# In the expert stage, TensorE's step goes from gate, up, weight spread, down to gate, weight spread, down, up

## The chip, the cores and the metric

The kernel runs on one core of a Trainium2 chip. The metric is the device time of one launch in microseconds (us), as the median of several runs. The profile is that of one execution on the same core.

## What is computed

Four layers follow each other, each added to its input x of 16 sequences, 128 rows and 256 columns: a grouped cross attention, a mixture of experts, a latent cross attention, and a feed-forward layer on quantised numbers. The change lies in the mixture of experts alone:

```python
logits = jnp.einsum('bsh,eh->bse', x, classifier_w)          # 12 routes, 8 of them experts
probs = softmax(logits)
_, idx = jax.lax.top_k(probs + e_score_correction_bias, 2)
rw = jnp.take_along_axis(probs, idx, axis=-1) * 1.5
w_full = jnp.sum(one_hot(idx, 12) * rw[..., None], axis=-2)
g = jnp.einsum('bsh,eih->bsei', x, gate_w)
u = jnp.einsum('bsh,eih->bsei', x, up_w)
expert_out = jnp.einsum('bsei,ehi->bseh', jax.nn.silu(g) * u, down_w)
out = jnp.einsum('bse,bseh->bsh', w_full[..., :8], expert_out)
out = out + x * jnp.sum(w_full[..., 8:], axis=-1, keepdims=True)
```

Here x is the normalised input of the layer.

## The kernel before

The function `routed_experts` holds the stage. Its work is cut into 32 units: 4 groups of 4 sequences (512 rows), and in each group the 8 experts. Unit u is expert x of group j, with u = 8j + x. A unit passes through all engines:

- TensorE makes the gate and the up product of the unit (L881), six matmuls of 512 columns each: two halves of the 256 columns, times three products, since every operand is split in a high and a low part.
- ScalarE takes the silu of the gate product (`gated`, L937). VectorE multiplies it with the up product (`inner`, L979).
- TensorE spreads the routing weight of this expert over the 128 partitions (L895). VectorE multiplies it in (`h`, L1008, in the helper `hidden`).
- ScalarE rounds h to its high part (`ht`, L945), GpSimd subtracts that to get the low part (`ht`, L1088).
- TensorE makes the down products (L904), 12 matmuls of 256 columns, which add up over the 8 experts of a group in `down_ps`. At the end of a group VectorE adds them to x (L1001).

The order of the work is written out by hand: each engine has a function `step(u, j, x)` and runs it for u = 0 to 34. Steps 0 to 7 are written out, steps 8 to 31 are a hardware loop over the groups, and three steps drain the pipeline. Each engine executes in this order and waits on semaphores. In step u TensorE makes gate and up of unit u, the spread of unit u - 2, the down products of unit u - 3, and in even steps three transposes of quantised weights for the last layer (L914). In step u VectorE makes `inner` of unit u - 1, then a piece of that quantisation, then `h` of unit u - 2. The piece is `block_powers` in an even step (four instructions, L1023 to L1027) and `shift` in an odd one (five instructions on 384 columns, L1034 to L1041). In step u GpSimd makes the low part of unit u - 3, then its piece of the quantisation (L1095 in even steps, L1099 in odd ones, the latter after `shift`), and then work for later stages: a rotation of the context in the steps with x = 0 to 4 (L1121 to L1131) and a scaling of x with x = 6 and 7 (L1072, L1075).

TensorE waits for these: `inner_made` before the gate product, so that the PSUM bank of unit u - 2 is free; `h_lo` (the low part) before the down products; `h_made` before the spread, since the spread's bank has only one copy. `inner` waits for `gated_made` and `up_made`.

The routing weights of a group have to be turned before they can be spread: `routes(g)` (L868) transposes them on TensorE into the spread's bank, ScalarE copies them (L929), VectorE subtracts for the low part (L968), and the spread waits for `w_lo`. This happens in step 1 for group 0 and in steps 3, 4 and 5 for groups 1 to 3, between the gate and the up product.

```python
if inside(u, UNITS):
    wait(pe, inner_made, u - 1)
    for w, out, made in ((0, gate_ps[par], gate_made), (2 * FFN, up_ps[par], up_made)):
        if first and u in (3, 4, 5) and made is up_made:
            routes(u - 2)
```

Of the kernel before, what the change touches and what calls it, by code (L numbers as in the profile page):

```python
# [24 lines left out]
B, S, E = 16, 128, 256  # L25
CE = 64
EPS = 1e-5
HALVES = E // 128
GROUPS = B // 4
PRODUCTS = ((0, 0), (0, 1), (1, 0))  # L30
# [10 lines left out]
EXPERTS, ZERO, INTER = 8, 4, 128  # L41
# [9 lines left out]
FFN, MX = 1024, 32  # L51
# [5 lines left out]
def wait(engine, semaphore, value):  # L57

    if isinstance(value, int) and value <= 0:
        return  # L60
    engine.wait_ge(semaphore, value)


def inside(n, count):

    return not isinstance(n, int) or 0 <= n < count
# [10 lines left out]
def run_of(ap, j, count=4):  # L77

    return ap.rearrange("p (j b) s -> p j b s", b=count)[:, j, :, :]
# [690 lines left out]
def routed_experts(nc, m, d):  # L770
# [7 lines left out]
    with ExitStack() as scope:  # L778
# [3 lines left out]
        UNITS = GROUPS * EXPERTS  # L782
# [7 lines left out]
        ht = [sb(f"ht{i}", [INTER, 2, N], F32R) for i in range(2)]  # L790
# [5 lines left out]
        gate_ps, up_ps = [m.bank(0), m.bank(2)], [m.bank(1), m.bank(3)]  # L796
        down_ps = m.ps[:, 4:6, :].rearrange("s c (b e) -> s (c b) e", b=2)
# [7 lines left out]
        w_at = lambda part, c, width: m.wsplit[:, part, c:c + width]  # L805
# [5 lines left out]
        gate_made, up_made, gated_made, inner_made = (sem(n) for n in ("e_gate", "e_up", "e_gated", "e_inner"))  # L811
        weight_spread, h_made, h_hi, h_lo, down_made = (sem(n) for n in ("e_weight", "e_h", "e_h_hi", "e_h_lo", "e_down"))
        x_made, parts_made, stats_made, var_made = (sem(n) for n in ("e_x", "e_parts", "e_stats", "e_var"))
# [11 lines left out]
        def steps(engine, step):  # L825

            def group(j):
                for x in range(EXPERTS):
                    step(EXPERTS * j + x, j, x)

            group(0)
            with engine.Fori(1, GROUPS) as j:
                group(j)
            for x in range(3):
                step(UNITS + x, GROUPS, x)

        @block.sync
        def _(sp):
            sp.dma_start(m.kv_cos[:, :], d["kv_cos"]).then_inc(m.rope_loaded, 16)
            sp.dma_start(m.kv_sin[:, :], d["kv_sin"]).then_inc(m.rope_loaded, 16)  # L840
            sp.dma_start(m.kvt_cos[:, :], d["kvt_cos"]).then_inc(m.rope_loaded, 16)
            sp.dma_start(m.kvt_sin[:, :], d["kvt_sin"]).then_inc(m.rope_loaded, 16)
            sp.dma_start(m.ctx_t[:, :, :, :], d["ctx_t"]).then_inc(m.rope_loaded, 16)
            sp.dma_start(m.rope[:, :, :], d["rope"]).then_inc(m.rope_loaded, 16)

            def load(c2, j, buf):

                wait(sp, mx_made, 2 * c2 - 2)
                sp.dma_start(raw[buf][:, :, :], d["mx"][c2, :, :, :]).then_inc(mx_loaded[buf], 16)

            load(0, 0, 0)
            load(1, 0, 1)
            with sp.Fori(1, GROUPS) as j:
                load(2 * j, j, 0)
                load(2 * j + 1, j, 1)
            load_wide(sp, m, d, 0)

        @block.tensor
        def _(pe):
            def routes(g):  # L860
                if g == 0:
                    pe.wait_ge(route, ROUTE_STEPS)
                else:
                    pe.wait_ge(h_made, g)
                if g == 3:
                    pe.wait_ge(mx_kept, 1)
                for s in range(4):
                    t = pe.transpose(weights_turned_ps[:, s * S:(s + 1) * S], weights[:, 4 * g + s, :], m.ident[:, :])  # L868
                t.then_inc(w_turned, 1)

            def step(u, j, x):
                par, old = x % 2, 1 - x % 2
                first = isinstance(u, int) and u < UNITS
                if inside(u, UNITS):
                    wait(pe, inner_made, u - 1)
                    for w, out, made in ((0, gate_ps[par], gate_made), (2 * FFN, up_ps[par], up_made)):
                        if first and u in (3, 4, 5) and made is up_made:
                            routes(u - 2)
                        for k in range(HALVES):
                            for q, (pw, py) in enumerate(PRODUCTS):  # L880
                                t = pe.matmul(out, w_at(pw, w + k * EXPERTS * INTER + x * INTER, INTER),  # L881
                                              run_of(m.yt[:, py, k, :, :], j).rearrange("p b s -> p (b s)"),
                                              start=(k == 0 and q == 0), stop=(k == HALVES - 1 and q == 2))
                        t.then_inc(made, 1)
                if first and u == 1:
                    routes(0)
                if inside(u - 2, UNITS):
                    if first and u == 2:
                        pe.wait_ge(m.selected, 1)
                    if first and 2 <= u <= 5:  # L890
                        pe.wait_ge(w_lo, u - 1)
                    wait(pe, h_made, u - 2)
                    if x % 2:
                        wait(pe, mx_kept, 4 * j + x // 2 - 1)
                    pe.matmul(weight_ps, select[:, (x - 2) % EXPERTS, :],  # L895
                              weights_t[:, j if x >= 2 else j - 1, :], start=True, stop=True).then_inc(weight_spread, 1)
                if inside(u - 3, UNITS):
                    expert = (x - 3) % EXPERTS
                    pe.wait_ge(h_lo, u - 2)
                    if expert == 0:  # L900
                        wait(pe, x_made, j)
                    for q, (ph, pw) in enumerate(PRODUCTS):
                        for s in range(4):
                            t = pe.matmul(down_ps[:, s, :], ht[old][:, ph, s * S:(s + 1) * S],  # L904
                                          w_at(pw, 4 * FFN + expert * E, E),
                                          start=(expert == 0 and q == 0 and s % 2 == 0),
                                          stop=(expert == EXPERTS - 1 and q == 2 and s % 2 == 1))
                    t.then_inc(down_made, 1)
                if x % 2 == 0 and inside(u - 2 - LEAD, UNITS):
                    c = 4 * j + x // 2 - 1  # L910
                    pe.wait_ge(mx_made, c)
                    pe.wait_ge(h_made, u - 1 if inside(u - 2, UNITS) else UNITS)
                    for i in range(3):
                        t = pe.transpose(mx_ps[:, i * 128:(i + 1) * 128],  # L914
                                         quantised[(x // 2) % 2][:, i * 128:(i + 1) * 128], m.ident16[:, :])
                    t.then_inc(mx_turned, 1)

            for b in range(B):
                t = pe.transpose(logit_ps[:, b, :], m.logits_t[:, b // 4, (b % 4) * S:(b % 4 + 1) * S],
                                 m.ident[0:ROUTES, 0:ROUTES])  # L920
            t.then_inc(logits_turned, 1)
            steps(pe, step)

        @block.scalar
# [1280 lines left out]
```

## Time and profile before

| | |
|---|---|
| median of 3 runs | 818.46 us (818.2 to 818.87) |
| the profiled execution's own time | 819.62 us |
| span of its profile, first to last instruction | 817.8 us |
| its mean granted TensorE clock | 0.981 |
| TensorE matmul busy | 749.2 us (92% of the span) |
| VectorE busy | 594.5 us (73%) |
| GpSimd busy | 567.1 us (69%) |
| ScalarE busy | 403.1 us (49%) |
| expert stage, first gate product to last transposes | 172.32 to 336.03 us |

The profiled execution took 1.16 us more than the median, and its span leaves 1.82 us around the first and the last instruction. Shares of the whole span say little on one stage; the stage is read in the trace from 172 to 337 us. In the rows, PE is TensorE's matmuls, PEld its weight loads, DVE is VectorE, ACT ScalarE, POOL GpSimd.

### The profile page before, as it was taken

How to read it: one execution, taken by the hardware profiler on the slowest of the kernel's cores; microseconds unless marked ns; L12 is line 12 of the kernel's file. 1: busy time of each engine (PE TensorE's matmuls, PEld its weight loads, DVE VectorE, ACT ScalarE, POOL GpSimd, SP SyncE). 2: the span in 40 equal slices, each digit the busy share in tenths (PEclk: the TensorE clock that was granted, in tenths of full speed). 3: DMA queues.
4: the chain of work that ended last, by engine and by line, in shares of the span. 5: the costliest groups of instructions: out<-in, count | busy, mean ns of one | idle time of the engine just before them, and what ended most of it. 6: DMA issues, size and time to landing. Idle time of an engine off the chain costs nothing. (4 is left out here: it accounts for less than half of the span.)

```text
span 817.8 us, 14830 instructions
## 1 busy us (share of the span) xinstructions
PE 749.2 (92%) x4801; PEld 538.7 (66%) x4808; DVE 594.5 (73%) x1087; ACT 403.1 (49%) x1068; POOL 567.1 (69%) x590
## 2 busy tenths in 40 slices
PE   3999999878999998789999999999999999876786
PEld 2555555457888887656877777777777777653464
DVE  5888889856777878656465575886678675749994
ACT  1688887532323323226455545545444545454463
POOL 5677776425867667465656878787887787817996
PEclk9999999979999999989999999999999999997999
DMA  9300000040100010322200000000000000000001
GB/s 249 122 2 0 0 0 1 1 171 1 39 20 19 19 58 0 107 76 70 84 15 1 1 1 2 2 1 1 1 1 1 2 1 1 1 2 7 26 34 39
DMA packets 8763, 24.12 MB, mean 29 GB/s; under 512 B 1711, under 2 KB 5167, under 8 KB 8087
## 3 DMA queue, kind: packets, MB, share of 16 engines
q1 hardware_dynamic: 8154, 23.28, 8.6%
q8 instruction: 33, 0.54, 0.3%
q14 instruction: 27, 0.22, 0.1%
q10 hardware_dynamic: 549, 0.08, 0.1%
HBM read 21.26 MB, written 2.10 MB: 29 GB/s over the span
## 5 line engine op out<-in xcount | busy, mean ns | idle before, releaser
L1622 POOL TENSOR_TENSOR q<-turned 64x512 f32<-64x512 f32 x128 | 168.0, 1312 | 25.7 <-DVE turned L1548 9.5
L1299 PE MATMUL ps<-l_yt,a 128*128 128x512 f32 x576 | 146.0, 404 | 2.1 <-ACT p L1445 1.7
L1299 PEld LDWEIGHTS ps<-l_yt,a 128*128 128x128 f32 x576 | 106.2, 190 | 27.8 <-issue 4.7
L1609 POOL TENSOR_TENSOR p<-p,l_inverse 128x512 f32<-128x512 f32 x64 | 66.9, 1047 | 74.7 <-DVE l_inverse L1570 74.3
L1445 ACT ACTIVATE p<-ps,l_negmax 128x128 f32<-128x128 f32 x256 | 91.1, 382 | 43.2 <-DVE l_negmax L1539 43.1
L1548 DVE TENSOR_TENSOR turned<-ps,rope 128x1024 f32<-128x1024 f32 x64 | 78.1, 1221 | 45.0 <-PE ps L1299 42.3
L881 PE MATMUL ps<-yt_experts,wsplit 128*128 (+1 forms) x384 | 97.1, 401 | 0.2 <-DVE inner L979 0.2
L467 DVE TENSOR_REDUCE negmax<-ps 128x4 f32<-128x512 f32 x128 | 85.2, 686 | 14.8 <-PE ps L290 13.4
L881 PEld LDWEIGHTS ps<-yt_experts,wsplit 128*128 128x128 f32 x384 | 71.1, 192 | 14.4 <-DVE inner L979 0.5
L1539 DVE TENSOR_REDUCE l_negmax<-ps 128x4 f32<-128x512 f32 x64 | 41.2, 686 | 44.3 <-PE ps L1357 44.1
L383 ACT ACTIVATE pt<-ps 128x512 f32<-128x512 f32 x128 | 69.9, 599 | 5.2 <-PE ps L312 3.5
L1462 ACT ACTIVATE qs<-ps 128x512 f32<-128x512 f32 x32 | 19.1, 597 | 98.4 <-PE ps L1315 98.4
L1560 DVE TENSOR_TENSOR turned<-ps,rope 64x512 f32<-64x512 f32 (+1 forms) x96 | 65.6, 683 | 2.0 <-PE ps L1299 0.7
L290 PE MATMUL ps<-bd,qt 96*128 96x512 f32 x128 | 59.0, 485 | 4.0 <-DVE negmax L467 2.0
L1339 PE MATMUL ps<-wc,cs 128*128 128x256 f32 x384 | 61.1, 295 | 1.4 <-DVE cs L1576 1.4
L904 PE MATMUL ps<-wsplit,ht 128*128 128x256 f32 x384 | 51.7, 284 | 9.3 <-POOL ht L1088 9.3
L904 PEld LDWEIGHTS ps<-wsplit,ht 128*128 128x128 f32 x384 | 49.7, 191 | 13.7 <-POOL ht L1088 11.8
L1445 ACT ACTIVATION_READ_ACCUMULATOR p<-ps,l_negmax 128x1 f32 x256 | 56.9, 222 | 0.0
L945 ACT ACTIVATE ht<-h 128x512 fp32r<-128x512 f32 x32 | 20.2, 632 | 70.2 <-DVE h L1008 68.2
L290 PEld LDWEIGHTS ps<-bd,qt 96*128 96x128 f32 x128 | 25.7, 201 | 40.1 <-DVE negmax L467 26.2
L312 PE MATMUL ps<-qt,bd 104*128 104x512 f32 x128 | 51.9, 432 | 0.0
L1339 PEld LDWEIGHTS ps<-wc,cs 128*128 128x128 f32 x384 | 49.6, 189 | 1.7 <-DVE cs L1576 1.7
(214 smaller groups left out, 1566.5 us busy)
## 6 DMA issues: line engine op xcount, KB each, us to landing
wide<-in_wide SPq DMA_DIRECT2D x8, 768.0 KB, 4.4
mx_raw<-in_mx SPq DMA_DIRECT2D x8, 384.0 KB, 3.1
x<-in_x SPq DMA_DIRECT2D x4, 512.0 KB, 9.1
ctx_t<-in_ctx_t SPq DMA_DIRECT2D x1, 2048.0 KB, 7.9
out<-x SPq DMA_DIRECT2D x16, 128.0 KB, 1.7
narrow<-in_narrow SPq DMA_DIRECT2D x8, 192.0 KB, 2.8
ktraw<-in_ctx_rows SPq DMA_DIRECT2D x1, 1248.0 KB
wraw<-in_gate SPq DMA_DIRECT2D x1, 1024.0 KB, 18.8
```

The costliest lines, as they stand in the source:

```text
L290: pe.matmul(scores[k % 2], qt[par][0:QROWS, half, g, :], bd[par][0:QROWS, half, :, :].rearrange("p k t -> p (k t)"), start=True, stop=True ...
L383: act.activation(pt[i][:, :], scores_t[i % 3], ACT.Exp, scale=scale).then_inc(exp_made, 1)
L467: dve.tensor_reduce(negmax[par][:, g, half * KV4:(half + 1) * KV4], scores[k % 2].rearrange("s (k t) -> s k t", k=KV4), AX.X, ALU.max, neg ...
L881: t = pe.matmul(out, w_at(pw, w + k * EXPERTS * INTER + x * INTER, INTER), run_of(m.yt[:, py, k, :, :], j).rearrange("p b s -> p (b s)"), ...
L904: t = pe.matmul(down_ps[:, s, :], ht[old][:, ph, s * S:(s + 1) * S], w_at(pw, 4 * FFN + expert * E, E), start=(expert == 0 and q == 0 and ...
L1299: out = pe.matmul(tile_bank(n, k), a[i][:, pa, kin, k * 128:(k + 1) * 128], yt[j % 2][:, py, kin, :, :].rearrange("p b s -> p (b s)"), sta ...
L1339: t = pe.matmul(proj_ps[:, half, s * E:(s + 1) * E], cs[n % 2][:, pc, (2 * half + s) * S:(2 * half + s + 1) * S], wc[:, pw, i, :], start=( ...
L1445: t = act.activation(p[:, head, s, :], scores_bank(n, head)[:, s * S:(s + 1) * S], ACT.Exp, bias=negmax[:, head, s:s + 1], accum_out=total ...
L1548: dve.tensor_tensor(turned[:, 2 * k:2 * k + 2, :].rearrange("p t (b s) -> p t b s", b=4), spread(tile_bank(n, k).rearrange("p (b s) -> p b ...
L1560: r = dve.tensor_tensor(turned[out_rows, k, :].rearrange("p (b s) -> p b s", b=4), tile_bank(n, 2)[in_rows, :].rearrange("p (b s) -> p b s ...
L1609: pool.tensor_tensor(p[:, head, :, :], p[:, head, :, :], spread(inverse[:, head, :], 2, S), ALU.mult).then_inc(normed[head], 1)
L1622: t = pool.tensor_tensor(out[rows[(head + half) % 2], head, :], turned[rows[head], half, :], turned[rows[head], 2 + half, :], ALU.add)
```

## The change

TensorE's step has another order. Gate and up are no longer neighbours: the spread of unit u - 2 and the down products of unit u - 3 come between them, and the up products close the step, ahead of the transposes of even steps. Each product keeps its waits and its semaphore. Step 1 keeps gate, up and then `routes(0)`. The three later `routes` stand where they stood, behind the gate product, but what follows them is the spread, no longer the up product. The code of VectorE, ScalarE, GpSimd and the DMA queues is the same.

```diff
             def step(u, j, x):
-                par, old = x % 2, 1 - x % 2
                 first = isinstance(u, int) and u < UNITS
                 if inside(u, UNITS):
                     wait(pe, inner_made, u - 1)
-                    for w, out, made in ((0, gate_ps[par], gate_made), (2 * FFN, up_ps[par], up_made)):
-                        if first and u in (3, 4, 5) and made is up_made:
-                            routes(u - 2)
-                        for k in range(HALVES):
...
-                        t.then_inc(made, 1)
+                    products(u, j, x, 0, gate_ps[x % 2], gate_made)
                 if first and u == 1:
+                    products(u, j, x, 2 * FFN, up_ps[1], up_made)
                     routes(0)
+                if first and u in (3, 4, 5):
+                    routes(u - 2)
                 if inside(u - 2, UNITS):
...
                     pe.matmul(weight_ps, select[:, (x - 2) % EXPERTS, :],
                               weights_t[:, j if x >= 2 else j - 1, :], start=True, stop=True).then_inc(weight_spread, 1)
                 if inside(u - 3, UNITS):
-                    expert = (x - 3) % EXPERTS
-                    pe.wait_ge(h_lo, u - 2)
...
+                    down(u, j, x)
+                if inside(u, UNITS) and not (first and u == 1):
+                    products(u, j, x, 2 * FFN, up_ps[x % 2], up_made)
+                turn_tiles(u, j, x)
```

`products`, `down` and `turn_tiles` hold the old statements of the six products, the down products and the transposes, unchanged.

The first place is TensorE in the loop over the groups: the down products that end the even step x = 0, its transposes, and the odd step x = 1. L881 is gate and up, L895 the spread, L904 the down products, L914 the transposes; the brackets name the semaphores waited for (e_h_lo is the low part, e_inner is `inner`). Before:

```order
L904 MATMUL ps<-wsplit,ht 128x256 [waits e_h_lo]
L904 MATMUL ps<-wsplit,ht 128x256 x11
L911 ISA
L914 MATMUL ps<-ident,mx_quantised 128x128 [waits e_h,mx_made]
L914 MATMUL ps<-ident,mx_quantised 128x128 x2
L881 MATMUL ps<-yt_experts,wsplit 128x512 [waits e_inner]
L881 MATMUL ps<-yt_experts,wsplit 128x512 x11
L895 MATMUL ps<-r_weights_t,r_select 128x512 [waits mx_kept,e_h]
L904 MATMUL ps<-wsplit,ht 128x256 [waits e_h_lo]
L904 MATMUL ps<-wsplit,ht 128x256 x11
```

The same place in the changed kernel, where L901 is gate or up, L889 the spread, L914 the down products and L927 the transposes:

```order
L914 MATMUL ps<-wsplit,ht 128x256 [waits e_h_lo]
L914 MATMUL ps<-wsplit,ht 128x256 x11
L901 MATMUL ps<-yt_experts,wsplit 128x512 x6
L924 ISA
L927 MATMUL ps<-ident,mx_quantised 128x128 [waits e_h,mx_made]
L927 MATMUL ps<-ident,mx_quantised 128x128 x2
L901 MATMUL ps<-yt_experts,wsplit 128x512 [waits e_inner]
L901 MATMUL ps<-yt_experts,wsplit 128x512 x5
L889 MATMUL ps<-r_weights_t,r_select 128x512 [waits mx_kept,e_h]
L914 MATMUL ps<-wsplit,ht 128x256 [waits e_h_lo]
L914 MATMUL ps<-wsplit,ht 128x256 x11
L901 MATMUL ps<-yt_experts,wsplit 128x512 x6
```

The six up products moved from ahead of the spread to behind the down products, so they stand behind the wait for the low part.

The second place is TensorE in step 3, where `routes(1)` (L868) turns the weights of group 1 and the spread waits for them (w_lo2). Before:

```order
L881 MATMUL ps<-yt_experts,wsplit 128x512 [waits e_inner]
L881 MATMUL ps<-yt_experts,wsplit 128x512 x5
L868 MATMUL ps<-ident,r_weights 128x128 [waits e_h]
L868 MATMUL ps<-ident,r_weights 128x128 x3
L881 MATMUL ps<-yt_experts,wsplit 128x512 x6
L895 MATMUL ps<-r_weights_t,r_select 128x512 [waits e_h,w_lo2]
L904 MATMUL ps<-wsplit,ht 128x256 [waits e_h_lo]
L904 MATMUL ps<-wsplit,ht 128x256 x11
```

In the changed kernel:

```order
L901 MATMUL ps<-yt_experts,wsplit 128x512 [waits e_inner]
L901 MATMUL ps<-yt_experts,wsplit 128x512 x5
L868 MATMUL ps<-ident,r_weights 128x128 [waits e_h]
L868 MATMUL ps<-ident,r_weights 128x128 x3
L889 MATMUL ps<-r_weights_t,r_select 128x512 [waits e_h,w_lo2]
L914 MATMUL ps<-wsplit,ht 128x256 [waits e_h_lo]
L914 MATMUL ps<-wsplit,ht 128x256 x11
L901 MATMUL ps<-yt_experts,wsplit 128x512 x6
```

Between the transposes of the weights and the spread that waits for their copies, the six up products are gone; they follow the down products. Steps 4 and 5 move in the same way.

## Rows read from the trace of the kernel before

**Rows 1.** Windows: length, busy us of PE, PEld, DVE, ACT, POOL, clock, DMA share, GB/s.

```profile
172.30:174.00 1.70, 1.70 (x5) 1.39 (x5) 1.07 (x4) 0.77 (x2) 0.00 (x0) 0.50 0.20 55
...
324.10:337.70 13.60, 7.46 (x57) 6.49 (x55) 8.62 (x26) 2.87 (x5) 10.54 (x9) 1.00 0.00 0
```

**Rows 2.** Timeline, TensorE: start us, us, engine, line, op, out<-in, xcount [idle before <-releaser].

```profile
208.69 3.01 PE L881 MATMUL ps<-yt_experts,wsplit 128*128 128x512 f32 x12
...
211.77 1.60 PE L904 MATMUL ps<-wsplit,ht 128*128 128x256 f32 x12
...
213.20 2.91 PE L881 MATMUL ps<-yt_experts,wsplit 128*128 x12
...
215.95 0.39 PE L895 MATMUL ps<-r_weights_t,r_select 128*128 x1
...
226.83 3.01 PE L881 MATMUL ps<-yt_experts,wsplit 128*128 x12
...
264.27 3.01 PE L881 MATMUL ps<-yt_experts,wsplit 128*128 x12
```

**Rows 3.** Timeline, TensorE: down products that wait for the low part, and transposes.

```profile
207.00 1.70 PE L904 MATMUL ps<-wsplit,ht 128*128 128x256 f32 x12 [0.81 <-POOL ht L1088]
...
208.54 0.34 PE L914 MATMUL ps<-ident,mx_quantised 128*128 128x128 bf16 x3
...
235.38 1.70 PE L904 MATMUL ps<-wsplit,ht 128*128 128x256 f32 x12 [0.91 <-POOL ht L1088]
```

**Rows 4.** Timeline: ScalarE, VectorE and GpSimd on the way from a product to `ht`.

```profile
201.28 0.56 DVE L1034 TENSOR_SCALAR ps<-mx_raw 128x384 uint32<-128x384 uint32 x1
...
203.66 0.55 DVE L1041 SCALAR_TENSOR_TENSOR mx_raw<-mx_raw,ps 128x384 f32<-128x384 f32 x1
204.25 0.69 DVE L1008 TENSOR_TENSOR h<-inner,ps 128x512 f32<-128x512 f32 x1
...
205.68 1.27 POOL L1088 TENSOR_TENSOR ht<-h,ht 128x512 fp32r<-128x512 f32 x1 [0.55 <-ACT ht L945]
...
210.36 0.60 ACT L937 ACTIVATE gated<-ps 128x512 f32<-128x512 f32 x1 [0.95 <-PE ps L881]
...
320.44 0.69 DVE L979 TENSOR_TENSOR inner<-gated,ps 128x512 f32<-128x512 f32 x1
...
321.05 0.55 DVE L1034 TENSOR_SCALAR ps<-mx_raw 128x384 uint32<-128x384 uint32 x1
```

**Rows 5.** Timeline: GpSimd in odd steps (x = 7, 1 and 3).

```profile
204.29 0.83 POOL L1099 TENSOR_TENSOR mx_quantised<-mx_raw,mx_scale 128x384 bf16<-128x384 f32 x1 [4.11 <-DVE mx_raw L1041]
...
212.16 1.89 POOL L1075 TENSOR_TENSOR x<-x,r_offset 128x1024 f32<-128x1024 f32 x1
...
214.02 1.29 POOL L1088 TENSOR_TENSOR ht<-h,ht 128x512 fp32r<-128x512 f32 x1
...
220.99 0.83 POOL L1099 TENSOR_TENSOR mx_quantised<-mx_raw,mx_scale 128x384 bf16<-128x384 f32 x1 [1.72 <-DVE mx_raw L1041]
...
221.78 0.74 POOL L1125 TENSOR_TENSOR kvr<-kvr,kvs  x1
...
222.67 1.29 POOL L1088 TENSOR_TENSOR ht<-h,ht 128x512 fp32r<-128x512 f32 x1
...
270.05 1.30 POOL L1129 TENSOR_TENSOR ctx_t<-ctx_t,kvt_sin 128x512 f32 x1
...
271.51 1.27 POOL L1088 TENSOR_TENSOR ht<-h,ht 128x512 fp32r<-128x512 f32 x1 [0.16 <-POOL ctx_t L1129]
```

**Rows 6.** Timeline, TensorE in steps 3 and 4, and the products of step 31.

```profile
190.57 1.69 PE L904 MATMUL ps<-wsplit,ht 128*128 128x256 f32 x12 [1.62 <-POOL ht L1088]
...
193.50 0.60 PE L868 MATMUL ps<-ident,r_weights 128*128 128x128 f32 x4
...
195.55 0.50 PE L895 MATMUL ps<-r_weights_t,r_select 128*128 128x512 f32 x1
...
321.01 3.01 PE L881 MATMUL ps<-yt_experts,wsplit 128*128 x12
```

More of the change, by code:

```diff
@@ L875, in step @@
                     wait(pe, inner_made, u - 1)
-                    for w, out, made in ((0, gate_ps[par], gate_made), (2 * FFN, up_ps[par], up_made)):
-                        if first and u in (3, 4, 5) and made is up_made:
-                            routes(u - 2)
-                        for k in range(HALVES):
[L880 to L883, printed above, removed]
-                        t.then_inc(made, 1)
+                    products(u, j, x, 0, gate_ps[x % 2], gate_made)
                 if first and u == 1:
+                    products(u, j, x, 2 * FFN, up_ps[1], up_made)
                     routes(0)
+                if first and u in (3, 4, 5):
+                    routes(u - 2)
                 if inside(u - 2, UNITS):
@@ L897, in step, with products, down, turn_tiles @@
                 if inside(u - 3, UNITS):
-                    expert = (x - 3) % EXPERTS
-                    pe.wait_ge(h_lo, u - 2)
[L900 to L908, printed above, removed]
+                    down(u, j, x)
+                if inside(u, UNITS) and not (first and u == 1):
+                    products(u, j, x, 2 * FFN, up_ps[x % 2], up_made)
+                turn_tiles(u, j, x)
+            def products(u, j, x, w, out, made):
+                for k in range(HALVES):
+                    for q, (pw, py) in enumerate(PRODUCTS):
+                        t = pe.matmul(out, w_at(pw, w + k * EXPERTS * INTER + x * INTER, INTER),
+                                      run_of(m.yt[:, py, k, :, :], j).rearrange("p b s -> p (b s)"),
+                                      start=(k == 0 and q == 0), stop=(k == HALVES - 1 and q == 2))
+                t.then_inc(made, 1)
+            def down(u, j, x):
+                expert, old = (x - 3) % EXPERTS, 1 - x % 2
+                pe.wait_ge(h_lo, u - 2)
+                if expert == 0:
+                    wait(pe, x_made, j)
+                for q, (ph, pw) in enumerate(PRODUCTS):
+                    for s in range(4):
+                        t = pe.matmul(down_ps[:, s, :], ht[old][:, ph, s * S:(s + 1) * S],
+                                      w_at(pw, 4 * FFN + expert * E, E),
+                                      start=(expert == 0 and q == 0 and s % 2 == 0),
+                                      stop=(expert == EXPERTS - 1 and q == 2 and s % 2 == 1))
+                t.then_inc(down_made, 1)
+            def turn_tiles(u, j, x):
                 if x % 2 == 0 and inside(u - 2 - LEAD, UNITS):
```

## The prediction

> **What bounds the kernel now.** I began with the busy times of the page, but they are means over four layers, so I went on to the windows, to find the expert stage and its clock, and then to the timeline of TensorE, where a step can be measured from product to product. The reader is to see there that TensorE sets the pace. From 208.69 to 226.83 us lie four steps, that is two pairs of an odd and an even step, without an idle row between them [rows 2]: 18.14 us, 9.07 per pair. A full group of eight steps takes 264.27 - 226.83 = 37.44 us, and four pairs at full pace 36.28, so a group loses only 1.16 us to waits. That loss has one place: the down products in the step with x = 4 wait 0.91 us for GpSimd's low part [rows 3]. So anything that puts a new wait into a step is paid in full, three times in the loop, and anything that takes a wait away can bring back at most 1.16 us per group.
>
> The parts of a step, from the same rows: twelve products take 215.95 - 213.20 = 2.75 us to the start of the spread, hence six take 1.38; the down products take 213.20 - 211.77 = 1.43 [rows 2]; transposes and what follows them 208.69 - 208.54 = 0.15 [rows 2, 3].
>
> **The change, part by part.** No instruction is added or removed. TensorE's work per pair stays 9.07 us. What moves is when its consumers get their input.
>
> *The low part is needed 1.38 us earlier in a step*, because the up products no longer run ahead of the down products. The spread moves forward by the same 1.38 us, so the distance from a spread to the down products of the same unit is still one step. In an even step VectorE's quantisation piece is short, `h` follows the spread, and nothing is lost.
>
> *The up product ends 1.43 us of down products and a spread later in its step.* VectorE begins each step with `inner` of the unit before, which needs that up product, and VectorE works in order. Before, `inner` was ready long ago; now it waits for the end of TensorE's step, and in an odd step the five instructions of `shift` and then `h` come behind it. That makes a ring, which I add up from one up product to the up product two steps later:
>
> - From the start of six products to their consumer: 210.36 - 208.69 = 1.67 (ScalarE's silu behind the gate product; VectorE behind the up product has no such row and is taken as equal) [rows 2, 4].
> - `inner` until `shift` starts: 321.05 - 320.44 = 0.61 [rows 4].
> - `shift`, first start to last end: 203.66 + 0.55 - 201.28 = 2.93, and 0.04 to `h` [rows 4].
> - `h` through ScalarE to the low part's start on GpSimd: 205.68 - 204.25 = 1.43 [rows 4].
> - The low part until the down products start: 207.00 - 205.68 = 1.32 [rows 3, 4].
> - Down products after such a wait, until the next TensorE instruction: 208.54 - 207.00 = 1.54 [rows 3].
>
> The sum is 9.54 us. The pair lasts 9.07 where TensorE alone sets it, so each pair becomes 0.47 us longer, and the wait appears at the down products of every even step.
>
> *GpSimd adds to it.* Between `shift` and the low part it has its own work in its order: the quantisation product 0.08 after `shift` ends, 0.79 until the next instruction, and then the work for later stages [rows 4, 5]. By way of VectorE and ScalarE it is 0.04 + 1.43 = 1.47 us from the end of `shift` to the low part. By way of GpSimd it is 0.87 plus: 1.86 at x = 7 (212.16 to 214.02), 0.89 at x = 1 (221.78 to 222.67), 1.46 at x = 3 (270.05 to 271.51), and nothing at x = 5. The longer way counts: +1.26, +0.29, +0.86 and 0.
>
> Per group: 4 x 0.47 + 1.26 + 0.29 + 0.86 = 4.29 us. The old wait at x = 4 does not come on top, as it is part of the new one there; subtract 1.16. Net +3.1 per group, and +9.4 for three groups (the waits fall into steps 8 to 30).
>
> *The first group* pays differently. In steps 3, 4 and 5 the spread waits for weights that have just been turned: 195.55 - 193.50 = 2.05 us from the transposes to the spread [rows 6]. Before, 1.38 us of up products lay in this time; now nothing does, and they follow later. That is 1.38 per step. In step 3 it costs nothing in the end: the down products there waited 1.62 us for the low part [rows 6], and `h` of unit 0, whose spread comes 1.38 earlier in step 2, now brings that forward. Steps 4 and 5 pay 2 x 1.38 = +2.8. Bounds: none of the three hidden 4.1, two hidden 1.4. In step 2 the gate product still covers the turning of group 0's weights; I take 0, at most 2.05 - 1.38 = 0.7.
>
> *The tail.* Step 31 still has an up product, so `shift` there moves as in the loop. It started 321.05 - 321.01 = 0.04 after the gate product [rows 4, 6]; now it starts 1.67 - 1.38 - 0.15 + 0.61 = 0.75 after it. The last units hang on this chain alone: +0.7, between 0 and 1.5.
>
> The sum: 9.4 + 2.8 + 0.7 = +12.9 us. The profiled execution's own 819.62 us would become 832.5, and the median of 818.46 becomes 831.4, since the profiled execution stands 1.16 above it. The range of this case: the ring's links are good to some 0.15 us per pair, which is 1.8 for twelve pairs; with the bounds of first group and tail this is 827.5 to 835.5.
>
> *A rule weighed against the rows.* Down products that had to wait show 1.70 us, those that had not 1.60 [rows 2, 3], and take 1.54 instead of 1.43 to the next instruction: the first weight load lies open. The Trainium skill, page "TensorE: Matmul & The Clock Gate", in the table that opens it, says that TensorE's queue can pull weight loads ahead of matmuls in flight. By that rule the twelve waits would each be 0.11 us cheaper, 1.3 us in all, and the result 830.1. I keep the row's value: here the low part is itself the weight that is loaded, so its load cannot pass the wait.
>
> **The rivals.**
>
> *VectorE's ring alone.* If GpSimd's low part did not come behind its other work, only the 0.47 per pair would be paid: 3 x (4 x 0.47 - 1.16) + 2.8 + 0.7 = +5.7, 824.1 us. Against it stands that the offset row ends and the low part follows at once [rows 5], so GpSimd's order already decides there; for it, that GpSimd's late work may be absorbed if TensorE's step is stretched anyway. 5%.
>
> *Not slower: the old wait goes and no new one comes.* At x = 2 VectorE adds the finished group to x, and that is what made the 0.91 us wait two steps later. The down products now end 1.38 us earlier in the step, so this addition no longer delays `inner`. If the ring is shorter than 9.07, the loop gains 3 x 1.16 = 3.5 us, the first group costs 2.8, and the tail nothing: 817.8 us; with the turned weights hidden too, 815.0. The point that decides is the ring: 0.47 us of 9.54 would have to be missing, for instance because VectorE sees the up product much sooner than ScalarE sees the gate product. That is more than any link can be off by these rows. 5%, with 3% inside the noise and 2% faster.
>
> *The clock falls.* At the stage's beginning the granted clock was 0.50, which is 1.2 GHz [rows 1], after the transposes and small products of the stage before; five products took 1.70 us in that window, against 0.23 us each at the full clock [rows 2]. New waits of 1 to 2 us could let it fall. If one step in each of the twelve pairs ran its twelve products at 0.34 instead of 0.23 us, this would add 12 x 1.3 = 16 us: 847 us. Against it stands the last window of the stage, where TensorE is busy 7.46 of 13.60 us and the granted clock is still 1.00, which is 2.4 GHz [rows 1]. The same page of the Trainium skill, Part 1, states that the clock is throttled by default and that activity releases it, at these two levels only; the windows agree on the levels (0.50 and 1.00). 4%.
>
> **How the numbers follow.** 86% for the forecast, whose time I give: 831.4 us. The range is 825.0 to 837.0: the forecast's own 827.5 to 835.5, widened by what TensorE's and GpSimd's rows leave open on both sides, and it leaves out the three rivals, 14% together, and some 6% of the forecast's own edges. A measurement of this kernel tells 0.2% from no change, that is 816.8 to 820.1 us. Faster by more has 2%, within it 3%, slower by more 95%.
>
> **What would show it.** In the changed profile the down products of even steps should wait for GpSimd's low part in each of the four pairs of a group, most in the step with x = 0 (some 1.6 us beyond full pace), next x = 4 (1.2), x = 2 (0.6) and x = 6 (0.3); odd steps should wait nowhere. VectorE's `inner` should show waits for the up product where it had none. A loop group should last near 40.6 us instead of 37.44, the spread in steps 4 and 5 should wait about 1.5 us for the turned weights, and the clock should stay at 1.00. I am wrong if `inner` starts well before the end of TensorE's step, or if the low part is ready before the down products although `shift` came late.

## The result, and the profile after

The changed kernel takes 833.01 us (median of 4 runs, 831.43 to 834.15) against 818.33 for the kernel before (4 runs): a ratio of 1.0178, 95% interval 1.0156 to 1.0201, slower by 14.7 us. 831.4 had been forecast, in a range of 825.0 to 837.0. The profiled execution took 834.04 us with a span of 832.2, 14.4 more than the span before.

First the loop, on TensorE: the down products that wait, and the transposes that end each even step. These rows are the timeline of the changed kernel; they answer to [rows 2, 3].

```profile
220.56 1.69 PE L914 MATMUL ps<-wsplit,ht 128*128 128x256 f32 x12 [1.40 <-POOL ht L1101]
...
223.48 0.34 PE L927 MATMUL ps<-ident,mx_quantised 128*128 128x128 bf16 x3
...
230.38 1.70 PE L914 MATMUL ps<-wsplit,ht 128*128 128x256 f32 x12 [0.48 <-POOL ht L1101]
...
233.31 0.34 PE L927 MATMUL ps<-ident,mx_quantised 128*128 128x128 bf16 x3
...
240.80 1.70 PE L914 MATMUL ps<-wsplit,ht 128*128 128x256 f32 x12 [1.08 <-POOL ht L1101]
...
243.73 0.34 PE L927 MATMUL ps<-ident,mx_quantised 128*128 128x128 bf16 x3
...
250.32 1.70 PE L914 MATMUL ps<-wsplit,ht 128*128 128x256 f32 x12 [0.17 <-POOL ht L1101]
...
253.25 0.34 PE L927 MATMUL ps<-ident,mx_quantised 128*128 128x128 bf16 x3
...
261.07 1.70 PE L914 MATMUL ps<-wsplit,ht 128*128 128x256 f32 x12 [1.41 <-POOL ht L1101]
...
264.00 0.34 PE L927 MATMUL ps<-ident,mx_quantised 128*128 128x128 bf16 x3
```

Every even step waits for the low part, no odd step does. From transposes to transposes a pair takes 9.83 us (x = 2), 10.42 (x = 4), 9.52 (x = 6) and 10.75 (x = 0 of the next group) where it took 9.07 before, and 10.24 at x = 4; a group takes 264.00 - 223.48 = 40.52 us instead of 37.44. The waits of VectorE in the loop point to the cause. The numbers are us in total, times, longest; first the changed kernel from 217 to 335 us:

```profile
DVE inner L992 <- PE ps L901: 26.2, 21, 3.2
```

And the kernel before, from 203 to 337 us, where `inner` is not in the list:

```profile
DVE h L1008 <- PE ps L895: 18.1, 19, 1.9
```

Before, VectorE waited for the spread; now `inner` waits for the up product. One pair in full, x = 5 and 6, from the timeline of all engines:

```profile
242.34 1.55 PE L901 MATMUL ps<-yt_experts,wsplit 128*128 x6
...
243.99 0.69 DVE L992 TENSOR_TENSOR inner<-gated,ps 128x512 f32<-128x512 f32 x1 [2.37 <-PE ps L901]
...
244.59 0.55 DVE L1047 TENSOR_SCALAR ps<-mx_raw 128x384 uint32<-128x384 uint32 x1
...
246.96 0.55 DVE L1054 SCALAR_TENSOR_TENSOR mx_raw<-mx_raw,ps 128x384 f32<-128x384 f32 x1
...
247.55 0.69 DVE L1021 TENSOR_TENSOR h<-inner,ps 128x512 f32<-128x512 f32 x1
...
248.98 1.28 POOL L1101 TENSOR_TENSOR ht<-h,ht 128x512 fp32r<-128x512 f32 x1 [0.55 <-ACT ht L958]
...
251.86 1.55 PE L901 MATMUL ps<-yt_experts,wsplit 128*128 x6
...
256.48 0.55 DVE L1054 SCALAR_TENSOR_TENSOR mx_raw<-mx_raw,ps 128x384 f32<-128x384 f32 x1
...
257.11 0.83 POOL L1112 TENSOR_TENSOR mx_quantised<-mx_raw,mx_scale 128x384 bf16<-128x384 f32 x1 [2.40 <-DVE mx_raw L1054]
...
257.90 1.89 POOL L1088 TENSOR_TENSOR x<-x,r_offset  x1
...
259.75 1.26 POOL L1101 TENSOR_TENSOR ht<-h,ht 128x512 fp32r<-128x512 f32 x1
```

That is the ring of the prediction, link by link: up product to `inner` 1.65 us, to `shift` 0.60, through `shift` 2.92, to `h` 0.04, to the low part 1.43, to the down products 1.34 (250.32), to the next up product 1.54. Together 9.52, the distance from 242.34 to 251.86. The last four rows show GpSimd's order in the odd step x = 7: from the end of `shift` (257.03) it is 2.72 us to the low part by way of the quantisation and the offset, where VectorE and ScalarE take 1.47.

The first group is read in windows: start and end, length, busy us of PE, PEld, DVE, ACT, POOL, granted clock, DMA share, GB/s. These are of the changed kernel:

```profile
179.91:183.50 3.59, 3.59 (x11) 2.81 (x12) 2.14 (x4) 0.60 (x1) 2.95 (x7) 0.52 0.68 271
183.50:189.37 5.87, 4.06 (x19) 2.93 (x18) 3.94 (x9) 2.32 (x4) 3.39 (x4) 1.00 0.00 0
189.37:194.00 4.63, 4.63 (x19) 4.10 (x20) 2.65 (x5) 0.63 (x1) 2.41 (x3) 0.63 0.00 0
194.00:212.74 18.74, 15.04 (x87) 12.11 (x86) 10.47 (x21) 5.16 (x9) 9.28 (x9) 1.00 0.08 22
```

From the first transposes of weights (179.91) to the second turning of quantised weights (212.74) it takes 32.83 us; before, the same stretch took 27.58 (180.96 to 208.54). The granted clock is near its lower level, 1.2 GHz, twice in it. Before, it was low too, but earlier: 0.50 from 170 to 176 us, at the stage's beginning, where the changed kernel's execution had 1.00.

The difference of the two spans by stage: before the first transposes -1.05 us, the first group +5.25, three groups +9.21, the tail up to the last transposes +0.68, and all that follows +0.31. The sum is 14.4. So 1.05 us of the two spans differ before the moved work begins.

### The profile page after: what moved, and what is told of

Read it like the earlier page. It is cut to its first block and busy times, and to the rows that moved or that the text cites. A ratio compares the mean times of both kernels' runs of the same rounds, so it can differ in the third digit from the quotient of the medians.

```text
span 832.2 us, 14830 instructions
## 1 busy us (share of the span) xinstructions
PE 752.1 (90%) x4801; PEld 537.9 (65%) x4808; DVE 594.3 (71%) x1087; ACT 403.7 (49%) x1068; POOL 567.1 (68%) x590
## 5 line engine op out<-in xcount | busy, mean ns | idle before, releaser
L901 PE MATMUL ps<-yt_experts,wsplit 128*128 (+1 forms) x384 | 99.3, 403 | 0.0
L901 PEld LDWEIGHTS ps<-yt_experts,wsplit 128*128 128x128 f32 x384 | 70.7, 193 | 13.1 <-DVE inner L992 0.2
L914 PE MATMUL ps<-wsplit,ht 128*128 128x256 f32 x384 | 53.3, 289 | 15.3 <-POOL ht L1101 15.3
L914 PEld LDWEIGHTS ps<-wsplit,ht 128*128 128x128 f32 x384 | 49.5, 192 | 22.9 <-POOL ht L1101 21.6
```

## The experiments

Six experiments test the ring, GpSimd's order and the first group; a repeat shows what the clock does by itself; three more look for a version that beats both kernels.

**New order in the loop and the tail alone.** The first eight steps keep the old order.

```diff
-                if first and u == 1:
+                if first and u in (3, 4, 5):
+                    routes(u - 2)
+                if inside(u, UNITS) and first:
                     products(u, j, x, 2 * FFN, up_ps[x % 2], up_made)
+                if first and u == 1:
                     routes(0)
...
-                if inside(u, UNITS) and not (first and u == 1):
+                if inside(u, UNITS) and not first:
```

> The first eight steps keep the old order, the loop and the tail have the new one. If the loss is the ring (up product, inner, shift, h, low part, down products) with GpSimd's later work, a loop group lasts 40.5 us as in the changed kernel, the loop and the tail cost 9.4 + 0.7 us, and the time is 818.3 + 10.1 = 828.4 us. If most of the loss came from the first group (its waits for turned weights and what they do to the clock), the time is below 823 us.

Measured: 831.65 us, ratio 1.0161 (1.0113 to 1.0209). Its groups, here and below from the transposes of x = 4 to those of the next group, take 40.51 and 40.52 us, with the same four waits. Before's runs in this series scatter from 815.6 to 822.9, so the ratio's 9 to 17 us hold the expected 10.1 without fixing it; the trace shows the loop's part exactly.

**New order in steps 2 to 7 alone.** The condition `first` above becomes `not first or u == 1`.

> Only steps 2 to 7 have the new order, the loop has the old one. The sum of the prediction gives +2.8 us for them, 821.1 us, with loop groups of 37.44 us again. The changed kernel's trace shows the granted clock at 0.50 twice in its first group, after waits, and about 2.4 us more than the sum there: if the clock is part of the cost of the new order, this run shows a clock of 0.50 after the spread's waits in steps 3 to 5, and 822 to 824 us; if that was chance, 821 us.

Measured: 821.83 us, ratio 1.0030 (1.0006 to 1.0053), some 2.5 us. The loop is back at 37.42 and 37.45 us per group. The stretch of the first group (27.58 us before) takes 31.64 us, and the clock fell in it, behind the waits of step 3:

```profile
186.50:187.70 1.20, 1.20 (x10) 1.20 (x11) 1.13 (x3) 0.00 (x0) 0.00 (x0) 1.00 0.00 0
187.70:192.00 4.30, 4.30 (x16) 3.50 (x15) 2.21 (x4) 0.63 (x1) 3.27 (x3) 0.60 0.00 0
192.00:200.00 8.00, 6.34 (x39) 4.94 (x37) 3.20 (x7) 2.82 (x6) 3.42 (x4) 1.00 0.01 2
```

**Up before down.** In the loop: gate, spread, up, down. The first eight steps keep the old order, as in the first experiment.

```diff
+                if inside(u, UNITS) and not first:
+                    products(u, j, x, 2 * FFN, up_ps[x % 2], up_made)
                 if inside(u - 3, UNITS):
                     down(u, j, x)
-                if inside(u, UNITS) and not (first and u == 1):
-                    products(u, j, x, 2 * FFN, up_ps[x % 2], up_made)
```

> In the loop: gate, weight spread, up, down; the first eight steps are old. Gate and up are as far split as one spread, the spread is early, but the up product no longer stands behind the wait for the low part. By the ring theory the ring then closes only over three steps, 11.3 us against 13.6 us of TensorE's work, so no even step waits, VectorE's inner no longer waits, a group lasts 37.4 us and the time is 818.3 us, 1 us either way. If instead splitting gate from up, or making the spread early, is what costs, a group stays above 39 us and the time near 826 us.

Measured: 819.62 us, ratio 1.0017 (0.9994 to 1.0040). Its groups take 37.45 and 37.43 us, and from 217 to 320 us TensorE waits for the low part only where it did before:

```profile
233.68 1.69 PE L915 MATMUL ps<-wsplit,ht 128*128 128x256 f32 x12 [0.90 <-POOL ht L1102]
```

`inner` still waits for the up product here and there, 5.7 us in ten waits in that window, a wait that I had not expected; but the groups last no longer for it. So splitting gate from up and spreading the weight early cost nothing. What costs is the up product behind a wait that its own descendant ends.

**GpSimd's later work moved.** The changed kernel; the rotations of x = 1 and 3 and the offset of x = 7 come behind the low part of the next step.

```diff
+                if inside(u, UNITS) and x in (2, 4):
+                    rotate_context(pool, m, rotated, j, x - 1)
+                if x == 0 and inside(j - 1, GROUPS):
+                    scale_x(j - 1, 7)
...
-                if inside(u, UNITS) and x < ROTARY_STEPS:
+                if inside(u, UNITS) and x in (0, 2, 4):
                     rotate_context(pool, m, rotated, j, x)
-                if inside(u, UNITS) and x in (6, 7):
+                if inside(u, UNITS) and x == 6:
                     scale_x(j, x)
```

> The changed kernel, with GpSimd's later work of odd steps (rotation at x = 1 and 3, offset at x = 7) moved behind the low part of the next step. If GpSimd's order adds 1.26, 0.29 and 0.86 us per group to the ring, the waits of even steps all shrink to about 0.35 us, against 1.41, 0.47 and 1.08 now; as the moved work makes GpSimd's even steps fuller, up to 0.6 us per group may come back in odd steps. A group lasts 38.2 to 38.8 us instead of 40.5, the time falls by 5 to 7 us to 826 to 828. If GpSimd's order is not what adds, the time stays at 833.

Measured: 828.17 us, ratio 1.0114 (1.0063 to 1.0166). A group takes 38.39 us: three pairs of 9.50 to 9.53 and one of 9.82. The waits of 1.41, 0.48 and 1.08 us are gone; what is left is the bare ring and one new wait of 0.48 in the odd step x = 1, as the filled even step x = 0 delays its low part.

```profile
215.78 1.70 PE L914 MATMUL ps<-wsplit,ht 128*128 128x256 f32 x12 [0.17 <-POOL ht L1101]
...
221.20 1.69 PE L914 MATMUL ps<-wsplit,ht 128*128 128x256 f32 x12 [0.48 <-POOL ht L1101]
...
235.12 1.69 PE L914 MATMUL ps<-wsplit,ht 128*128 128x256 f32 x12 [0.17 <-POOL ht L1101]
```

So GpSimd's order is worth 40.52 - 38.39 = 2.13 us per group, net of the new wait. What is left over the kernel before, 38.39 - 37.44 = 0.95 us, is the ring and the new wait, less the old one.

**A shorter ring.** The changed kernel with four instructions in `shift` instead of five; the lower bound of 1 on the power is left out, so small elements of the last layer's weights are rounded otherwise.

```diff
-                then(2, dve.tensor_scalar(power, power, 1.0, None, ALU.max))
```

> The changed kernel with one of shift's five instructions left out (the lower bound of 1 on the power), 0.59 us in every odd step; the rounded weights of the last layer are different for small elements. By the ring theory each pair gets 0.59 shorter until TensorE's own 9.07 us bound it: 10.16 behind x = 7, 9.23 behind x = 1, 9.84 behind x = 3, 9.07 behind x = 5, a group of 38.3 us instead of 40.5, and 6.5 to 7.5 us less in all, 826 us. If VectorE's late inner did not set the pace, group and time stay.

Measured: 826.01 us, ratio 1.0079 (1.0056 to 1.0102). A group takes 38.34 us, in pairs of 10.16, 9.24, 9.85 and 9.08. The expected 10.16, 9.23, 9.84 and 9.07 are met within 0.01 us each, also where TensorE's own work takes over as the bound.

**The waits of steps 3 to 5 filled.** The changed kernel with six more products between the turned weights and the spread, the up product made once too often.

```diff
                 if first and u in (3, 4, 5):
                     routes(u - 2)
+                    products(u, j, x, 2 * FFN, up_ps[x % 2], None)
```

> The changed kernel with six more products in steps 3, 4 and 5, between the transposes of the weights and the spread: they make the up product once more than needed, into the bank that the true one overwrites later. They fill the 1.46 us in which TensorE waited there and add next to no time of their own. If those waits let the clock fall, the granted clock stays at 1.00 from the first spread on, and from the first transposes of weights to the second turning of quantised weights it takes 29.9 us as in the run with GpSimd's work moved, whose clock did not fall, against 32.8 in the changed kernel and 31.6 where only the first group has the new order; the time is 831 us. If the clock there is independent of these waits, the stretch at 0.50 shows up again.

Measured: 831.60 us, ratio 1.0155 (1.0123 to 1.0188).

```profile
178.14:181.50 3.36, 3.36 (x10) 2.62 (x11) 2.15 (x4) 0.60 (x1) 2.29 (x7) 0.52 0.75 303
...
186.00:200.00 14.00, 13.53 (x75) 10.64 (x74) 8.04 (x15) 3.89 (x8) 8.22 (x8) 1.00 0.00 1
200.00:209.46 9.46, 8.61 (x48) 6.76 (x47) 6.58 (x13) 1.92 (x4) 4.98 (x5) 1.00 0.14 42
```

From step 3 on the clock is at 1.00. The stretch takes 31.32 us, not 29.9: the clock was low in step 2 already, ahead of the filled waits, where TensorE had stood 2.91 us for the route tables. One profile can't tell whether the filling kept the clock up, since the next run did without it.

**The changed kernel again.**

> The changed kernel once more, for its first group: if the stretch at a clock of 0.50 in step 3 depends on where the waits fall, this execution may show it or not, and the time from the first transposes of weights to the second turning of quantised weights is either 31.5 to 32.9 us with it or 29.9 without. The loop groups are 40.5 us again.

One execution: 830.08 us, against 817.67 for before, 12.4 more. The loop is the same (40.52 and 40.53 us per group). The clock did not fall in the first group from step 2 on, and the stretch takes 30.06 us:

```profile
178.66:186.00 7.34, 5.73 (x27) 4.41 (x27) 5.23 (x11) 2.92 (x5) 5.47 (x10) 1.00 0.36 143
186.00:195.00 9.00, 7.12 (x42) 5.99 (x43) 6.49 (x14) 1.72 (x3) 4.66 (x5) 1.00 0.00 0
195.00:208.72 13.72, 11.47 (x66) 9.12 (x64) 7.47 (x15) 4.07 (x7) 7.87 (x8) 1.00 0.10 30
```

So the new order costs the first group 30.06 - 27.58 = 2.5 us, and the 2.8 us on top of it in the other execution came with the clock.

But the clock fell in the tail of this execution, in the third set of down products from the end and the one after it (0.50 from 340 to 344 us). Such a set takes 1.70 us where the clock is up:

```profile
338.12 2.51 PE L914 MATMUL ps<-wsplit,ht 128*128 128x256 f32 x12 [2.76 <-POOL ht L1101]
```

The tail took 16.59 us for it, against 15.85 in the first execution. The time of 12.4 us more holds that too.

**A version meant to beat both.** Old order in the first eight steps, gate, spread, up, down in the loop, and GpSimd's later work moved: the edits of the third and fourth experiment together.

> A version meant to be faster than both: the first eight steps old, in the loop gate, spread, up, down, and GpSimd's later work of odd steps moved behind the low part of the next step. The ring is open, and of the old kernel's one wait per group (0.91 us at x = 4), which comes by way of GpSimd's rotation, 0.86 us should go. A group lasts 36.6 to 36.9 us against 37.44 before, and with a shorter tail the time is 1.5 to 3 us below before, 816 us. If the moved work only moves the wait, it equals before.

Measured: 818.06 us, ratio 1.0004 (0.9991 to 1.0017): no difference, so the forecast of 1.5 to 3 us less failed. The loop did what it should, 36.60 us per group. But the tail took 15.8 us, against 15.2 before and 14.4 in the third experiment, for two reasons: the last group's offset now lay ahead of the last low parts, and the clock fell in the last down products (2.22 us from their start to the transposes, where a set at the full clock takes 1.54). In the first group the clock fell too, with the old order, after the old wait of step 3. By this profile the loop gave 2.5 us, and the first group and the tail took 1.4 and 0.7 back. The two sets of down products that met the low clock, in step 3 and at the end of the tail:

```profile
187.95 2.75 PE L915 MATMUL ps<-wsplit,ht 128*128 128x256 f32 x12 [1.43 <-POOL ht L1102]
...
330.89 2.41 PE L915 MATMUL ps<-wsplit,ht 128*128 128x256 f32 x12 [2.77 <-POOL ht L1102]
```

And the window around the first:

```profile
188.00:192.00 4.00, 4.00 (x17) 3.72 (x18) 2.26 (x4) 0.63 (x1) 2.44 (x3) 0.57 0.00 0
```

**The same with the last offset at the end of the tail.**

```diff
-                if x == 0 and inside(j - 1, GROUPS):
+                if (x == 2 and tail) or (x == 0 and inside(j - 1, GROUPS) and not tail):
                     scale_x(j - 1, 7)
```

> The version meant to be faster, with the last group's offset moved to the end of the tail, behind its last low part: in the version before, this offset lay ahead of the last two low parts, and the tail from the second last loop transposes on took 15.8 us against 15.2 in the kernel before. A group stays at 36.6 us, the tail falls to 13 to 14.5 us, and the time is 2.5 to 4.5 us below before, if the clock in the first group does not hide it: 814.5 to 816. If the ends of the stages shift so that the gain is given back later, the time equals before.

Measured: 816.75 us against 819.96, ratio 0.9964 (0.9946 to 0.9982), 3 us below before. The tail takes 14.6 us, a little more than expected, and again the clock fell in its last down products, which take 2.63 us to the transposes instead of 1.54:

```profile
328.17 2.83 PE L915 MATMUL ps<-wsplit,ht 128*128 128x256 f32 x12 [2.19 <-POOL ht L1103]
```

In the loop TensorE's products have no wait left, only its weight loads have (1.9 us in six places from 215 to 320 us); the window is one group:

```profile
215.43:252.03 36.60, 36.60 (x214) 31.61 (x212) 29.00 (x60) 11.65 (x20) 27.47 (x28) 1.00 0.07 23
```

**Old order on TensorE with GpSimd's work moved.** The same edit on the kernel before.

> The order of the kernel before on TensorE, with the same move of GpSimd's work. If the order gate, spread, up, down is of no use by itself, this lasts as long: a group of 36.6 us, 0.2 at most beside the version with both, and a tail up to 0.8 us longer, since the spread's early place shortened the tail by 0.75 us. If the early spread is needed for the gain, a group stays near 37.4 us.

Measured: 819.10 us, ratio 0.9996 (0.9978 to 1.0014). Its groups take 36.59 and 36.63 us and its tail 14.3, as in the version above: the loop's gain comes from GpSimd's order alone. The pair that ends with x = 4 shows it, in the kernel before and in this one, from transposes to transposes:

```profile
226.68 0.34 PE L914 MATMUL ps<-ident,mx_quantised 128*128 128x128 bf16 x3
...
236.92 0.34 PE L914 MATMUL ps<-ident,mx_quantised 128*128 128x128 bf16 x3
```

```profile
225.66 0.34 PE L914 MATMUL ps<-ident,mx_quantised 128*128 128x128 bf16 x3
...
235.03 0.33 PE L914 MATMUL ps<-ident,mx_quantised 128*128 128x128 bf16 x3
```

That is 10.24 us before and 9.37 here. Yet the time equals before. Its profile has the clock low in step 3 (0.51 from 189 to 192 us), which accounts for some 1.4 us of one execution. Against the version above the medians differ by 2.35 us, with an interval of 0.7 to 4.0 us worked out from the twelve runs of each. Some 0.8 us of it can be the tail: 14.3 us here without a fall of the clock, and an estimated 14.6 - 1.1 = 13.5 above without one. The rest is not settled.

## Why the prediction was right

**The ring.** Forecast 9.54 us per pair where nothing else adds, measured 9.52 in the changed kernel and 9.50 to 9.53 in three of the four pairs when GpSimd's work was moved. The link without a row of its own, from the up product to VectorE, was taken as 1.67 and is 1.65. That it is a ring and not the sum of the moved pieces is shown by the third experiment and by the one with a shorter ring: opened by putting up ahead of down, it vanished; shortened by one instruction, it shortened by just that until TensorE's 9.07 us held.

**GpSimd's order.** Forecast +1.26, +0.29, +0.86 and 0 us on top of the ring, measured pairs of 10.75, 9.83, 10.42 and 9.52, that is +1.23, +0.31, +0.90 and 0 over the bare ring. Moving the work took away 2.13 of the 2.4 us per group, and the rest came back as the one wait in an odd step.

**The group.** Forecast 40.6 us, measured 40.52; +9.4 for three groups, measured +9.21. The old wait of 0.91 us at x = 4 did not come on top: that pair has one wait of 1.08. The prediction, in its second rival, put this old wait down to VectorE's addition of the finished group at x = 2. The last experiment shows another cause: with the old order on TensorE and nothing moved but GpSimd's work, the pair falls from 10.24 to 9.37 us, so 0.87 of its 1.17 us over full pace came by way of GpSimd's order. The sum did not need the cause.

**The first group.** Forecast +2.8, measured +2.5 where the clock stayed up. Steps 2 and 3 cost nothing, as forecast: 12.55 us from the first transposes of weights to those of step 4 (178.66 to 191.21 in the second execution), 12.54 before. Steps 4 and 5 cost 1.09 and 1.39 us instead of 1.38 each; in step 4 the transposes of before had waited for `h`, and that wait is hidden now. This is the row of before:

```profile
197.63 0.33 PE L914 MATMUL ps<-ident,mx_quantised 128*128 128x128 bf16 x3 [0.15 <-DVE h L1008]
```

**The tail.** Forecast +0.7, measured +0.68 in the profiled execution, where the clock stayed at 1.00 in the tail. The step behind it is close to the forecast: `shift` of step 31 starts 0.70 us after the gate product (334.43 to 335.13), where 0.75 was forecast and the kernel before had 0.04. The second execution shows +1.42, with the fall of the clock in its tail.

The order's cost is then 9.21 + 2.5 + 0.68 = 12.4 us where the clock is up, against 12.9 forecast. That the second execution also took 12.4 us more than before's median is in part chance, as its tail shows; its three stages alone come to 2.48 + 9.26 + 1.42 = 13.2 us. The medians differ by 14.7.

**What was mis-sized.** In the profiled execution 14.4 us of span stand against the order's 12.4: the clock's two falls in the first group add 2.8 us, the time ahead of the stage takes 1.05 off, and 0.31 come behind the stage. For the medians no trace says what the 2.3 us beyond 12.4 are. The clock in the first group is one candidate, but not the only one: what follows the last transposes of the stage is the same code in all twelve profiles and took 481.0 to 485.0 us. So it is partly luck that the whole time came within 1.6 us of the forecast.

The rival that the clock falls was given 4% and priced as falling in every pair of the loop; there it stayed at 1.00 through all waits, as the last window of before had suggested. Its price was also read wrongly: 0.34 us for a product came from five products counted in a window of 1.70 us, but six products at the low clock take 2.70 us to the spread in the changed kernel, 0.45 each, so that its twelve steps would have cost about twice the 16 us:

```profile
180.79 2.86 PE L901 MATMUL ps<-yt_experts,wsplit 128*128 128x512 f32 x6
183.49 0.40 PE L889 MATMUL ps<-r_weights_t,r_select 128*128 128x512 f32 x1
```

In the first group the clock did fall, twice in the profiled execution, so the sign that it should stay at 1.00 failed there. This is not the new order's doing as such: of the eleven other profiles of this document the fall in step 3 shows in one with the new first group and in two with the old one, and the fall in step 2 in one of each. A fall costs this stretch some 1.4 to 1.6 us (28.99 against 27.58 us in old first groups, 31.64 against 30.06 in new ones), and in seven of the twelve profiles the clock fell in the tail as well. Whether the new waits make a fall likelier, these few profiles can't say.

The fall in step 2 goes with what lies ahead of it. In all three profiles that have it the clock had been at 1.00 at the stage's beginning, from 172 to 176 us, and TensorE then waited 2.87 to 2.91 us for the route tables. In the nine others the clock was low at the beginning, that wait was 0.40 to 1.29 us, and step 2 ran at 1.00. Up to the first transposes of weights the low clock cost nothing. Here are the gate and up products of steps 0 and 1 and these transposes, before:

```profile
172.32 7.52 PE L881 MATMUL ps<-yt_experts,wsplit 128*128 128x512 f32 x24
180.96 0.66 PE L868 MATMUL ps<-ident,r_weights 128*128 128x128 f32 x4 [1.11 <-DVE r_total L1052]
```

And in the changed kernel:

```profile
171.28 5.72 PE L901 MATMUL ps<-yt_experts,wsplit 128*128 128x512 f32 x24
179.91 1.06 PE L868 MATMUL ps<-ident,r_weights 128*128 128x128 f32 x4 [2.91 <-DVE r_total L1065]
```

From the first product to the transposes it is 8.64 and 8.63 us, since both wait for the same tables.

The Trainium skill, page "TensorE: Matmul & The Clock Gate", Part 1, says that the clock is throttled by default and released by activity, and the windows agree: all falls in the first group came behind a stretch in which TensorE had waited, for 1.6 to 2.9 us in all. But in step 3 the same waits left the clock up in other executions, so the rule gave a place, not a time.

The rule in the opening table of the same page of the Trainium skill, that weight loads are pulled ahead of matmuls in flight, would, as the prediction applied it, have made each waiting set of down products 0.11 us cheaper. The rows decide against it here: 1.54 us from 250.32 to 251.86, and 1.70 us busy, as before the change [rows 3].

One smaller slip: the prediction's bounds add up to 835.3 us at the upper edge, or 836.0 with step 2's 0.7, and not to 835.5. Nothing hangs on it.

## What to carry to other kernels

Moving work behind a wait can cost time in every turn when what ends this wait descends from the moved work. Follow the moved output through every engine's fixed order until it meets the wait again, add up the links, and compare the sum with the work of the engine that sets the pace; only a surplus costs (with the shorter ring the pair at x = 6 was back at 9.08 us). A small surplus (here 0.45 us in 9.07) comes back in every turn, and an engine that puts unrelated work between its input and the awaited output (here GpSimd, up to 1.23 us) adds to it. Work without a deadline belongs behind the output that somebody waits for, but look at the end of the loop too: the same move took part of the loop's gain back in the tail (15.8 us against 14.6 with the last piece at the very end).

A time that agrees with a forecast should be checked stage by stage: here a clock that fell in other places made two executions of one kernel differ by 2.8 us in one stage and by 0.7 the other way in another.

## What the runs showed of the hardware that I had not expected

The granted clock in the first group differs from execution to execution of one kernel (0.52 and 0.63 in two windows of one, 1.00 throughout in the next), with 32.83 against 30.06 us for the same stretch. Where it falls decides what it costs: nothing up to the first transposes of weights, where TensorE waits for the route tables anyway (8.64 us with a clock of 0.50 up to 176 us, 8.63 with 1.00), and 1.4 to 1.6 us in the steps behind them. And the links of the ring repeat to some 0.02 us: groups of 40.49 to 40.54 us in four profiles, whichever transposes they are counted from, so that a loop can be read from one trace although the times of whole runs scatter by 5 us.
